# The edge loop of a graph network: two of the four products of a quarter are computed ahead of the previous quarter's sums

## The chip, the cores and the metric

The kernel runs on one core of a Trainium2 chip. The metric is device time in microseconds. The engines are TensorE (PE in the profile; PEld is its load of the stationary operand), ScalarE (ACT), VectorE (DVE), GpSimd (POOL) and SyncE (SP), which issues DMAs. Each engine works through its own instructions strictly in the order written, and waits at a semaphore until another engine has counted it up.

## The reference

The network has 6250 nodes with 256 features and 200,000 edges, sorted by destination. A first layer is a weighted sum over the edges, a linear map and a norm, and gives `x1`. The second layer holds the work of the edge loop:

```
npj  = relu(layer_norm(x1 @ Wp + bp) * gp + betap)               # 20 per node
kron = outer(npj[src], npj[dst]).reshape(E, 400)                 # per edge
kron = relu(layer_norm(kron @ Wk + bk) * gk + betak)             # 256 per edge
kron_feat = segment_sum(kron, dst)
logits = relu([x1[dst], x1[src]] @ We + be)
a = softmax of logits over the edges of one dst
context = relu(segment_sum((x1 @ Wn + bn)[src] * a, dst))
```

A GRU cell, two norms and a linear map on the nodes end the network.

## The kernel before

After the first layer, a table row is stored for each node (`tab_dram`: its values, its `npj` and its half of the logit), and for each node as a destination the matrix `M[node]` of 21 x 257 (`m_dram`), so that an edge's linear result is its source's 21 numbers times the matrix of its destination.

**The tiles.** The edges are cut into tiles of 128 that belong to one bucket of six nodes. The left factor of a tile's product is 126 x 128: for each edge the 21 numbers, placed at its destination's share of 6 x 21. Sixteen tiles are a group (index `g`), a group has four quarters (`s` = 0 to 3) of four tiles. There are 164 groups, and a pass of the loop does four (`UN`), so that there are 41 passes; VectorE, ScalarE and TensorE end a pass between the quarters s=1 and s=2 of a group.

**One quarter, in order.** GpSimd gathers the sources' rows into `feat` (L804), into one of four buffers, each for a group; SyncE loads the 126 x 257 matrices into `m_ring` (L605), which holds 16, one group; the four of a quarter are loaded anew once TensorE has used all four (L602). VectorE multiplies the rows by the one-hots (`products`, L1507). TensorE turns the four tiles into one PSUM bank (`turn_products`, L1911; the profile puts every turn at L1720), ScalarE copies them to SBUF (`evacuate`, L960). TensorE then does a tile's product (`linear`, L1922; two instructions in the profile for each tile). ScalarE squares and sums its 256 columns for the variance (`square`, L970), then VectorE scales the tile out of PSUM into `hgb` (`scaled`, L1518). Only then is its bank free:

```
def bank_of(i):      return 2 if i == SG - 1 else 1 + i % 3
def last_in_bank(i): return {0: 4, 1: 2, 2: 4, SG - 1: 2}.get(i, 3)
...
past(pe, e_hg, t - last_in_bank(i) + 1)       # in linear(q, j)
```

So there are three banks for the products. Tile i of a group waits for the scaling of the tile three back; exceptions are tile 0, which waits for tile 12 of the group before, tile 1, which waits for tile 15 of the group before (two back), tile 2, which waits for tile 14, and tile 15, which waits for tile 13.

**Around the products.** A group later, VectorE clips the tiles (`clipped`, L1574, four in each quarter), which needs the deviations of the whole group: ScalarE computes them in quarter s=0 with a square root (`deviations`, L976), after a load of its function table. In s=1 it computes the exponentials of the slots (L985, L987), in s=2 those of the rows (L981); these need the other table, which is loaded in s=1. ScalarE also copies sums out of PSUM (`kron_rows`, L998, in s=1; `context_rows`, L993, in s=2). TensorE does the sums of the groups before in `softmax_products`:
- s=0: `turn_slot_logits`, which waits for the accumulators' update on VectorE (`add_slots`, L1562 and L1564); `sum_kron` (L1931); two `sum_context` (L1940)
- s=1: `sum_kron`; `turn_logits`, which waits for ScalarE's slot exponentials (L987)
- s=2: `sum_kron`
- s=3: `sum_kron`, two `sum_context`, `sum_slots` (L1969, L1970), which `add_slots` of the next quarter needs

The order is written out by hand for each engine. TensorE works quarter by quarter: products of tiles 0 and 1, turn of the next quarter's tiles, products of tiles 2 and 3, `softmax_products`. ScalarE: square of tile 0, copy of the turned tiles, square of tile 1, the extra function of this quarter, square of tile 2, exponentials, square of tile 3. VectorE: scaling of tiles 0 and 1, an extra step (`add_slots`, `slot_max` or `row_max`), the `products` of the quarter after next, scaling of tile 2, in s=3 the weighted one-hots, scaling of tile 3, the clipping. When a new group is taken up, which is at the head of s=2, `take_indices` (L1493) hands GpSimd the next indices.

Of the kernel before, what the change touches and what calls it, by code (L numbers as in the profile page):

```python
# [95 lines left out]
def gnn_program(nc, io, V, E, EP):  # L96
# [27 lines left out]
    with ExitStack() as ctx:  # L124
# [706 lines left out]
        def _(act):  # L831
# [123 lines left out]
            def evacuate(q):  # L955
                g, u, s = q
                n = g * ST + s
                act.wait_ge(e_t, n + 1)
                past(act, e_h, (n - 1) * G)
                nc.scalar.activation(prods_t[0:KM, s % 2, :], ps[0:KM, 0, :], ACT.Copy).then_inc(e_at, 1)  # L960

            def square(q, j):
                g, u, s = q
                i = s * G + j
                t = g * SG + i
                act.wait_ge(e_h, t + 1)
                past(act, e_sq, t - 1)
                if i == 0:
                    past(act, e_sd, g - 1)
                nc.scalar.activation(junk[:, i % 2, 0:D], ps[:, bank_of(i), 1:HC], ACT.Square, scale=1.0 / 16,  # L970
                                     accum_out=var[:, u % 2, i:i + 1]).then_inc(e_sq, 1)
# [28 lines left out]
            def edge_functions(it):  # L1000
                for k in range(UN * ST):
                    main, turned = quad(it, k - 2), quad(it, k - 1)
                    if main is None:
                        if turned is not None:
                            evacuate(turned)
                        continue
                    g, u, s = main
                    one, two = earlier(it, main, 1), earlier(it, main, 2)
                    square(main, 0)
                    if turned is not None:  # L1010
                        evacuate(turned)
                    square(main, 1)
                    if s == 0 and one is not None:
                        deviations(one[0], one[1] % 2)
                    if s == 1 and two is not None:
                        kron_rows(two[0])
                    if s == 2 and two is not None:
                        context_rows(two[0])
                    square(main, 2)
                    if s == 1 and two is not None:  # L1020
                        slot_exponentials(two[0], two[1] % 2)
                    if s == 2 and one is not None:
                        exponentials(one[0], one[1] % 2)
                    square(main, 3)

            edge_functions(0)
            with act.Fori(1, NS // UN) as it:
# [688 lines left out]
        def _(pe):  # L1716
# [274 lines left out]
            def edge_products(it):  # L1991
                for k in range(UN * ST):
                    turned, main = quad(it, k - 1), quad(it, k - 2)
                    if main is not None:
                        linear(main, 0)
                        linear(main, 1)
                    if turned is not None:
                        turn_products(turned)
                    if main is not None:
                        one, two = earlier(it, main, 1), earlier(it, main, 2)  # L2000
                        if main[2] == 2 and two is not None:
                            turn_slot_exponentials(two[0])
                        if main[2] == 3 and one is not None:
                            turn_exponentials(one[0])
                        linear(main, 2)
                        linear(main, 3)
                        softmax_products(it, main)

            pe.wait_ge(n_ma, 5 * NT)
# [97 lines left out]
```

## Time and profile before

| | |
|---|---|
| median of 3 runs | 9654.78 us (9641.32 to 9657.46) |
| profiled execution: its time / its span | 9633.56 / 9632.1 us |
| mean granted TensorE clock over the span | 0.851 |
| busy over the span | PE 72%, VectorE 64%, GpSimd 48%, ScalarE 39% |
| edge loop | about 4924 to 8773 us |
| middle of the edge loop, 3550 us | PE busy 2679.42, VectorE 2846.37, ScalarE 1975.19, GpSimd 2449.06 us |

The page gives the span in 40 slices, with the loop in slices 20 to 36. Busy time counts work and not waits. TensorE's durations are modelled and overlap, so that starts are the better measure there: the interval between two starts is what a group of instructions takes when nothing waits. A timeline merges neighbouring instructions of one line, and names at the end of a row what ended the idle time before it. In it, one tile's product is 2 instructions of L1922, one `sum_kron` 8 of L1931, one `sum_context` 8 of L1940, and one square an ACTIVATE and a short read of the accumulator.

### The profile page before, as it was taken

To read this page: it belongs to the slowest core of one execution; us is meant where nothing else is said; L and a number is where in the kernel's file an instruction comes from. 1 tells how busy PE (TensorE), PEld (TensorE's weight loads), DVE (VectorE), ACT (ScalarE), POOL (GpSimd) and SP (SyncE) were. 2 spreads that over 40 slices of the span, in tenths; PEclk is the share of its full clock that TensorE was granted. 3 is DMA by queue.
4 is the path that set the end of the run, shared out by engine and by line. 5 is a ranking of instruction groups with operands and counts; after the bars stand their busy time and mean duration, and the time that the engine had idled before them with its cause. 6 is when DMAs were issued, how large, how long until landed. Compare 5 with 4: busy or idle time off the path is not lost.

```text
span 9632.1 us, 164904 instructions
## 1 busy us (share of the span) xinstructions
PE 6952.0 (72%) x33451; PEld 4356.7 (45%) x33452; DVE 6131.5 (64%) x17345; ACT 3717.6 (39%) x10449; POOL 4601.2 (48%) x4921
## 2 busy tenths in 40 slices
PE   3164666666666799988877777777777777777887
PEld 3122444444444577743334444444444444444444
DVE  8894444444444566644458878787888778785555
ACT  0001444444444200023335555555555555553333
POOL 0003777787788400000047666676666666673000
PEclk9586777778787899965569999999999999999888
DMA  0003322222222388854467777777777777775000
GB/s 12 0 0 98 102 93 92 91 91 92 95 91 91 116 263 262 263 190 201 189 212 208 198 197 197 196 203 193 198 199 199 196 196 202 194 201 139 15 16 15
DMA packets 807298, 1398.58 MB, mean 145 GB/s; under 512 B 212677, under 2 KB 578772, under 8 KB 794073
## 3 DMA queue, kind: packets, MB, share of 16 engines
q1 hardware_dynamic: 588922, 797.11, 26.9%
q0 software_dynamic: 215360, 596.47, 21.9%
q14 instruction: 418, 3.42, 0.1%
q10 hardware_dynamic: 2586, 1.37, 0.1%
q8 instruction: 12, 0.20, 0.0%
HBM read 985.87 MB, written 434.45 MB: 147 GB/s over the span
## 4 chain that ended last, share of the span: by engine, by line
PE 32%; issue 22%; DVE 17%; POOL 9%; ACT 8%; DMA 7%; SPq 3%; DVEq 2%; ACTq 1%; POOLq 0%
POOL msg_dram L783 8%; PE ps L1922 7%; PE ps L1720 4%; PE ps L1823 4%; ACT junk L970 3%; PE ps L1940 3%; DMA arena_e<-msg_dram 3%; PE ps L1931 3%; DMA arena_n<-rec_dram 2%; PE ps L1838 2%; DVE arena_e L1574 2%; DVE arena_r L1256 2%; DVE arena_e L1518 2%; SPq L529 2%; ACT L985 1%
## 5 line engine op out<-in xcount | busy, mean ns | idle before, releaser
L804 POOL DMA_INDIRECT arena_n<-tab_dram,idxs x2624 | 2637.6, 1005 | 2831.1 <-DVE idxs L1493 1685.4
L783 POOL DMA_INDIRECT msg_dram<-arena_e,idxq x1760 | 1796.2, 1021 | 473.0 <-issue 467.5
L1922 PE MATMUL ps<-arena_n 126*128 126x257 f32 x5232 | 1686.8, 430 | 446.2 <-DVE arena_e L1518 444.7
L1812 PE MATMUL ps<-arena_n,arena_r 128*128 x3520 | 1252.2, 517 | 383.9 <-ACT arena_r L871 383.9
L970 ACT ACTIVATE junk<-ps 128x256 f32<-128x256 f32 x2616 | 995.7, 382 | 1309.4 <-PE ps L1922 1225.8
L1518 DVE TENSOR_TENSOR arena_e<-ps,gkx 128x257 f32<-128x257 f32 x2616 | 1068.5, 422 | 554.6 <-ACT junk L970 540.0
L1922 PEld LDWEIGHTS ps<-arena_n 126*128 126x128 f32 x5232 | 907.2, 203 | 939.3 <-DVE arena_e L1518 790.6
L1812 PEld LDWEIGHTS ps<-arena_n,arena_r 128*128 128x128 f32 x3520 | 864.8, 257 | 657.5 <-issue 502.7
L876 ACT ACTIVATE arena_e<-ps,recq 128x256 f32<-128x256 f32 x1760 | 809.8, 475 | 772.9 <-PE ps L1812 769.0
L1574 DVE SCALAR_TENSOR_TENSOR arena_e<-arena_e,rstd,nbetak_b 128x256 f32<-128x256 f32 x2608 | 1088.4, 480 | 5.7
L1720 PE MATMUL ps<-ident,arena_n 128*126 128x128 f32 (+1 forms) x3109 | 578.3, 294 | 509.9 <-DVE arena_r L1564 252.7
L1823 PE MATMUL ps<-arena_e,oh 128*128 128x256 f32 x3520 | 818.4, 387 | 85.8 <-DVE oh L1301 84.9
L1081 DVE TENSOR_SCALAR recq<-arena_n 128x16 f32 (+1 forms) x440 | 89.5, 203 | 1240.5 <-DMA msg_dram<-arena_e,idxq 1088.7
L1720 PEld LDWEIGHTS ps<-ident,arena_n 128*126 128x126 f32 (+1 forms) x3109 | 429.8, 150 | 759.3 <-issue 690.1
L1823 PEld LDWEIGHTS ps<-arena_e,oh 128*128 128x128 f32 x3520 | 641.0, 190 | 263.1 <-issue 157.3
L1720 PE MATMUL ps<-ident,oh 128*128 128x128 f32 x1760 | 333.5, 320 | 410.3 <-DVE oh L1301 408.3
L960 ACT ACTIVATE arena_n<-ps 126x512 f32<-126x512 f32 x655 | 390.9, 597 | 362.8 <-PE ps L1720 362.8
L970 ACT ACTIVATION_READ_ACCUMULATOR junk<-ps 128x1 f32 x2616 | 530.1, 203 | 0.0
L1720 PEld LDWEIGHTS ps<-ident,oh 128*128 128x128 f32 x1760 | 226.9, 161 | 614.1 <-DVE oh L1301 600.9
L1931 PE MATMUL ps<-arena_e,oh 128*32 128x257 f32 x5216 | 467.6, 404 | 2.3 <-DVE arena_e L1574 0.5
L871 ACT ACTIVATE arena_r<-ps 128x512 f32<-128x512 f32 x440 | 262.8, 597 | 518.9 <-PE ps L1720 517.5
L1507 DVE TENSOR_TENSOR arena_n<-arena_n,oh 128x504 f32<-128x504 f32 x656 | 445.4, 679 | 22.2 <-DMA arena_n<-tab_dram,idxs 18.9
(308 smaller groups left out, 8995.8 us busy)
## 6 DMA issues: line engine op xcount, KB each, us to landing
arena_n<-m_dram SPq DMA_DIRECT2D x2624, 126.5 KB
arena_e<-msg_dram SPq DMA_DIRECT2D x441, 514.0 KB, 4.5
m_dram<-arena_e SPq DMA_DIRECT2D x49, 1413.5 KB, 4.9
m_dram<-arena_e SPq DMA_DIRECT2D x49, 1285.0 KB, 4.5
arena_n<-tab_dram,idxs POOLq DMA_INDIRECT x2624
hist_dram<-arena_r SPq DMA_DIRECT2D x163, 253.0 KB
msg_dram<-arena_e,idxq POOLq DMA_INDIRECT x1760
arena_n<-rec_dram SPq DMA_DIRECT2D x444, 8.0 KB
```

The lines of the kernel that those rows point to most:

```text
L783: nc.gpsimd.indirect_dma_start(out=msg_dram, in_=msgs[:, u, j, :], in_offset=None, out_offset=bass.IndirectOffsetOnAxis(ap=idxq[:, u, j:j ...
L804: nc.gpsimd.indirect_dma_start(out=feat[:, u, i, :], out_offset=None, in_=tab_dram, in_offset=bass.IndirectOffsetOnAxis(ap=idxs[:, u, i:i ...
L876: nc.scalar.activation(msgs[:, u, j, 0:D], ps[:, 2 + j, 0:D], ACT.Copy, scale=recq[:, u, 4 * j + 2:4 * j + 3]).then_inc(m_msg, 1)
L970: nc.scalar.activation(junk[:, i % 2, 0:D], ps[:, bank_of(i), 1:HC], ACT.Square, scale=1.0 / 16, accum_out=var[:, u % 2, i:i + 1]).then_in ...
L1507: tt(prods[:, s % 2, :].rearrange("p (j n a) -> p j n a", j=G, n=BN), feat[:, u, s * G:(s + 1) * G, PS0:PS0 + KA].unsqueeze(2).broadcast_t ...
L1518: tt(hgb[:, u % 2, i, 0:HC], ps[:, bank_of(i), 0:HC], gkx[:, :], ALU.mult).then_inc(e_hg, 1)
L1574: stt(out=h, in0=h, scalar=rstd[:, u % 2, i:i + 1], in1=nbetak_b[:, :], op0=ALU.mult, op1=ALU.max).then_inc(e_clip, 1)
L1720: return nc.tensor.transpose(out, src, ident[:, :])
L1812: mm(ps[:, 2 + j, 0:D], oh_t[:, q, j * P:(j + 1) * P], at(x_all, nt[u], D, MSG), start=True, stop=True).then_inc(m_x, 1)
L1823: ins = mm(ps[:, q, 0:D], oh[:, q, j * P:(j + 1) * P], msgs[:, u, j, 0:D], start=(j == 0), stop=(j == G - 1))
L1922: mm(ps[:, bank_of(i), 0:HC], prods_t[0:KM, s % 2, j * P:(j + 1) * P], m_ring[0:KM, i, :], start=True, stop=True).then_inc(e_h, 1)
L1931: mm(ps[32 * j:32 * (j + 1), 4, 0:MSG], oh[:, u, 32 * i:32 * (i + 1)], hgb[:, u % 2, i, 1:1 + MSG], start=(s == 0), stop=(s == ST - 1)).th ...
```

## The change

TensorE does the products of tiles 0 and 1 of a quarter not at the quarter's start, but in the quarter before, behind the products of that quarter's tiles 2 and 3 and ahead of its `softmax_products`. ScalarE squares these two tiles at the end of the quarter before. VectorE's order, the number of instructions, the banks and all DMAs stay as they are.

```
@@ edge_functions(it), ScalarE
                     if main is None:
                         if turned is not None:
                             evacuate(turned)
+                            square(turned, 0)
+                            square(turned, 1)
                         continue
                     g, u, s = main
                     one, two = earlier(it, main, 1), earlier(it, main, 2)
-                    square(main, 0)
-                    if turned is not None:
-                        evacuate(turned)
-                    square(main, 1)
+                    evacuate(turned)
                     if s == 0 and one is not None:
                         deviations(one[0], one[1] % 2)
...
                     square(main, 3)
+                    square(turned, 0)
+                    square(turned, 1)
@@ edge_products(it), TensorE
                     turned, main = quad(it, k - 1), quad(it, k - 2)
-                    if main is not None:
-                        linear(main, 0)
-                        linear(main, 1)
                     if turned is not None:
                         turn_products(turned)
                     if main is not None:
...
                         linear(main, 2)
                         linear(main, 3)
+                    if turned is not None:
+                        linear(turned, 0)
+                        linear(turned, 1)
+                    if main is not None:
                         softmax_products(it, main)
```

`main` is the quarter whose tiles VectorE scales in this step, `turned` the next one.

## Rows read from the trace of the kernel before

**Rows 1.** The stretch view, in the middle of the edge loop.
```profile
5100.00:8650.00 3550.00, 2679.42 (x18174) 1665.50 (x18172) 2846.37 (x8177) 1975.19 (x6667) 2449.06 (x2439) 0.95 0.74 198
```

**Rows 2.** The waits, 5100 to 8650 us: total, times, longest.
```profile
DVE arena_e L1518 <- ACT junk L970: 494.2, 691, 2.5
...
DVE idxs L1493 <- issue: 125.4, 38, 4.4
```

**Rows 3.** The timeline of VectorE, one period: start, duration, instruction, idle before it.
```profile
7003.08 0.43 DVE L1518 TENSOR_TENSOR arena_e<-ps,gkx 128x257 f32<-128x257 f32 x1 [1.27 <-ACT junk L970]
7004.30 0.43 DVE L1518 TENSOR_TENSOR arena_e<-ps,gkx 128x257 f32<-128x257 f32 x1 [0.79 <-ACT junk L970]
...
7006.28 0.79 DVE L1518 TENSOR_TENSOR arena_e<-ps,gkx 128x257 f32<-128x257 f32 x2
...
7010.32 0.42 DVE L1518 TENSOR_TENSOR arena_e<-ps,gkx 128x257 f32<-128x257 f32 x1 [0.43 <-ACT junk L970]
...
7013.10 0.43 DVE L1518 TENSOR_TENSOR arena_e<-ps,gkx 128x257 f32<-128x257 f32 x1 [0.45 <-ACT junk L970]
...
7019.92 0.74 DVE L1518 TENSOR_TENSOR arena_e<-ps,gkx 128x257 f32<-128x257 f32 x2
...
7021.97 0.43 DVE L1518 TENSOR_TENSOR arena_e<-ps,gkx 128x257 f32<-128x257 f32 x1
...
7025.15 0.43 DVE L1518 TENSOR_TENSOR arena_e<-ps,gkx 128x257 f32<-128x257 f32 x1 [1.18 <-ACT junk L970]
```

**Rows 4.** The timeline of TensorE, the same period.
```profile
7005.77 0.30 PE L1720 MATMUL ps<-ident,arena_n 128*126 128x128 f32 x1 [1.51 <-DVE arena_r L1564]
7006.01 0.83 PE L1931 MATMUL ps<-arena_e,oh 128*32 128x257 f32 x8
...
7007.63 1.14 PE L1922 MATMUL ps<-arena_n 126*128 126x257 f32 x4
7008.61 0.60 PE L1720 MATMUL ps<-ident,arena_n 128*126 128x128 f32 x4
...
7020.72 0.70 PE L1922 MATMUL ps<-arena_n 126*128 126x257 f32 x2 [1.36 <-DVE arena_e L1518]
7021.35 0.64 PE L1931 MATMUL ps<-arena_e,oh 128*32 128x257 f32 x8
...
7023.79 1.03 PE L1922 MATMUL ps<-arena_n 126*128 126x257 f32 x4
```

**Rows 5.** The timeline of ScalarE, the same period.
```profile
7005.79 0.36 ACT L970 ACTIVATE junk<-ps 128x256 f32<-128x256 f32 x1
...
7009.33 0.60 ACT L960 ACTIVATE arena_n<-ps 126x512 f32<-126x512 f32 x1 [0.48 <-PE ps L1720]
...
7010.18 0.39 ACT L998 ACTIVATE arena_e<-ps 128x257 f32<-128x257 f32 x1
7010.44 0.40 ACT L970 ACTIVATE junk<-ps 128x256 f32<-128x256 f32 x1
...
7010.95 1.28 ACT L985 ACT_TABLE_LOAD   x1
...
7012.60 0.38 ACT L970 ACTIVATE junk<-ps 128x256 f32<-128x256 f32 x1
...
7025.38 0.60 ACT L960 ACTIVATE arena_n<-ps 126x512 f32<-126x512 f32 x1 [0.35 <-PE ps L1720]
7025.87 0.38 ACT L970 ACTIVATE junk<-ps 128x256 f32<-128x256 f32 x1
...
7026.36 1.28 ACT L976 ACT_TABLE_LOAD   x1
...
7027.86 0.36 ACT L970 ACTIVATE junk<-ps 128x256 f32<-128x256 f32 x1
```

**Rows 6.** The groups by line, 5100 to 8650 us: GpSimd's gathers.
```profile
L804 POOL DMA_INDIRECT arena_n<-tab_dram,idxs x2439 | 2450.8, 1005 | 1101.2 <-issue 663.2 <-PE ps L1940 418.2 <-DVE idxs L1493 19.8
```

**Rows 7.** The timeline of TensorE where the loop starts its next pass.
```profile
7080.85 2.08 PE L1922 MATMUL ps<-arena_n 126*128 126x257 f32 x4 [0.40 <-DVE arena_e L1518]
```

More of the change, by code:

```diff
@@ L1005, in edge_functions @@
                             evacuate(turned)
+                            square(turned, 0)
+                            square(turned, 1)
                         continue
@@ L1008, in edge_functions @@
                     one, two = earlier(it, main, 1), earlier(it, main, 2)
[L1009 to L1012, printed above, removed]
+                    evacuate(turned)
                     if s == 0 and one is not None:
@@ L1024, in edge_functions @@
                     square(main, 3)
+                    square(turned, 0)
+                    square(turned, 1)
             edge_functions(0)
@@ L1993, in edge_products @@
                     turned, main = quad(it, k - 1), quad(it, k - 2)
-                    if main is not None:
-                        linear(main, 0)
-                        linear(main, 1)
                     if turned is not None:
@@ L2006, in edge_products @@
                         linear(main, 3)
+                    if turned is not None:
+                        linear(turned, 0)
+                        linear(turned, 1)
+                    if main is not None:
                         softmax_products(it, main)
```

## The prediction

> **What bounds the kernel now.** The views were read in this order: the page's slices, which put the edge loop at 4924 to 8773 us; the stretch view of its middle; the waits there; then the timelines of three engines over one group, side by side. In 3550 us of the loop VectorE is busy 2846 us and TensorE 2679 us, at a granted clock of 0.95 [rows 1], so neither is full, and the loop is a chain that goes round between engines. The stretch holds 2439 gathers [rows 6], 16 to a group: 152.4 groups, 23.3 us each. VectorE, the fullest in its own work, waits 494 us for ScalarE's squares and 125 us (38 times, once a pass) at the head of a pass [rows 2].
>
> One group in steady state lasts 7025.15 - 7003.08 = 22.07 us [rows 3]. VectorE stands idle in it at tile 0 of s=0 (1.27 us), tile 1 of s=0 (0.79), tile 1 of s=1 (0.43), tile 3 of s=1 (0.45): 2.94 us. The first three come from one pattern: TensorE does those products only after the sums of the quarter before. From 7021.35 to 7023.79 it does the sums of s=3, and from 7005.77 to 7007.63 those of s=0 [rows 4], then come the products, the squares and the scalings. Quarters s=2 and s=3 have no wait on VectorE.
>
> **The change part by part.** It removes and adds no instruction. It moves two products of a quarter (TensorE) and their two squares (ScalarE). No DMA is moved, but SyncE's loads and GpSimd's gathers hang on TensorE's counts, see below. In the sum, times of s=0 stand one period (22.07 us) on, where that is needed.
>
> *Product of tile 0, ahead.* Its bank waits for the scaling of tile 1 of the same quarter (in s=3: tile 12), which is over when the product of tile 3 is. It costs its place, 0.44 us, which is not new work. Price 0.
>
> *Product of tile 1, ahead.* Here a wait comes. Its bank is that of tile 2 of the running quarter, and before s=0 that of tile 15, the group's last, which VectorE scales as the last before its clipping. The sums, the next turn, and the next products 2 and 3 are queued behind it on TensorE; ScalarE's copy waits for the turn, and VectorE for both. Step by step, for the two quarters in which it matters:
>
> s=3. The scaling of tile 15 starts at 7021.97 and takes 0.43 [rows 3]; a product that waited for a scaling started 0.06 after that one's end (7019.92 + 0.74 = 7020.66, then 7020.72), and what stood behind it began 0.63 later (7021.35) [rows 3, 4]. So the sums begin at 7021.97 + 0.43 + 0.06 + 0.63 = 7023.09 and not at 7021.35. They take 7023.79 - 7021.35 = 2.44, and the turn of the next quarter then follows at once, at 7025.53. Now two products (0.87, or 0.44 each) stand between, and it starts at 7024.66 (0.72 ahead of ScalarE's copy at 7025.38). The turn is 0.87 late. ScalarE's copy starts 0.72 after the turn (7008.61, 7009.33) [rows 4, 5]. There the change gives something back: behind the copy stood the square of tile 1, 7025.38 to 7026.36 up to the table load. Now the load follows the copy, which is 0.60 long, so at about 0.62 after its start: 0.36 saved. From the table load over the square root to the square of tile 2 it is 7027.86 - 7026.36 = 1.50, and the scaling of tile 2 follows 0.49 after its square (7005.79, 7006.28) [rows 3, 5]. It comes 0.51 later than now, and the waits of tiles 0 and 1 (2.06 us) have only moved to tile 2: VectorE has nothing else to do there but the accumulators and the multiplication.
>
> From scaling to scaling: 0.49 + 0.63 + 2.44 + 0.72 + 0.62 + 1.50 + 0.49 = **6.89 us** from tile 15 to tile 2 of s=0 (now 6.38).
>
> s=0. Tile 1 of s=1 waits for this scaling: 0.49 + 0.63. The sums then take 1.62 without a wait (7006.01 to 7007.63) and 1.86 with one (from 7005.77) [rows 4]; the turn of the slot logits now finds its operands ready, so I take 1.70. The turn, and 0.72 later the copy (0.49 to the next, 7025.38 to 7025.87), the rows' copy (0.26, 7010.18 to 7010.44), the square of tile 2 up to the table load (0.51), from there over two exponentials to the square of tile 3 (1.65, 7010.95 to 7012.60), and 0.50 to the scaling at 7013.10 [rows 3, 5]. Sum: 0.49 + 0.63 + 1.70 + 0.72 + 0.49 + 0.26 + 0.51 + 1.65 + 0.50 = **6.95 us**, where now it is 7013.10 - 7006.28 = 6.82.
>
> s=1, after tile 3, to tile 3 of s=3: VectorE works without a wait, 7021.97 - 7013.10 = **8.87 us** [rows 3], now and then. Products 0 and 1 of s=2 and s=3 wait too, but the turns there lie well ahead of VectorE's clipping, so nothing hangs on them. If that cover were gone, 0.4 to 1 us a quarter would be at stake.
>
> The round is 6.89 + 6.95 + 8.87 = 22.71 against 22.07: **+0.64 us a group**, and 163 groups have it: +104 us.
>
> *Against it: the extra waits.* Over the stretch VectorE waits 494.2 / 152.4 = 3.24 us a group, 0.30 more than the 2.94 of the steady group. Some of it comes from stretches at the lower clock: where the loop starts its next pass, four instructions took 2.08 us [rows 7] instead of about 1.03. In s=2 two products done ahead hide that; in s=3 and s=0 more of TensorE's work lies on the chain. Bounds 0 and -0.30; I take the middle, -0.15, or -25 us.
>
> *The transfers.* SyncE may reload a quarter of the ring once its fourth product is done. In s=1 that is before its scaling at 7013.10, and the first product of s=1 comes again at 7007.63 + 22.07 = 7029.70 [rows 3, 4]: over 16.6 us. In the new order it comes 2 to 3 us sooner, so some 14 us are left. The nearest rows of such size, in the page's list of DMA issues, are transfers of 514 KB that landed in 4.5 us; four matrices are 506 KB. Price 0; the cover is gone if four took over 14 us. GpSimd's gathers cost 2450.8 us and 663.2 us between them, for 152.4 groups 20.4 us a group [rows 6], less than 22.7. The heads of the passes, 3.3 us, hide TensorE's and ScalarE's own. Price 0.
>
> Sum: 104 - 25 = +79 us. For the profiled execution 9633.56 + 79 = about 9712; it stands 21 us under the median of the runs, to which the difference is added: 9654.78 + 79 = **9733 us**. Its bounds: each waiting product 0.44 instead of 0.63 (-0.38 a group), sums of s=0 at 1.62 or 1.86 (-0.08, +0.16), extra waits hidden whole or not at all (-0.15, +0.15): -0.61 to +0.31 a group about the +0.49, so -20 to +130 us.
>
> **The rivals.**
>
> *The banks are free in time (faster).* If product 1 did not wait, the sums of s=3 would start 0.87 after the product of tile 3, the turn would be where it is now, and ScalarE would save its 0.36. In s=0 the two products would lie in the wait for the accumulators, and the turn would come at 7007.7 instead of 7008.61; with 0.36 more saved there, the round is 1.3 us shorter: -212 us, 9443. It would have its place in the waits of products for VectorE. The two waits together cost about 1.97 us; the change gains from where they are below 1.3. Against it stand the scalings of tile 15 and tile 2, which lie 0.6 us and more behind TensorE [rows 3, 4]. Chance 0.08.
>
> *It cancels.* Waiting products restart at 0.44, and all the extra waits go: +0.64 - 0.38 - 0.30 = -0.04 a group, -7 us, 9648. A single row stands for the 0.63. Chance 0.14.
>
> *The clock falls more often.* The granted clock is 0.95 in the stretch [rows 1], so about a tenth of it is at 1.2 GHz. On the new chain lie 0.63 + 2.44 + 0.63 + 1.70 = 5.4 us of TensorE's work a group. The new order gives TensorE a wait in each quarter. If the lower clock held a fifth more of the time, it would be +1.1 us a group, +176 us on top: 9909; a tenth more, 9820. For it: rows 7, after a head. Against: the waits of now are as many (1.51, 1.36 us) [rows 4], and the clock stayed. Chance 0.07. The Trainium skill, "TensorE: Matmul & The Clock Gate", section "HAM oscillation — how this bites in real kernels", says that a loop whose waits starve TensorE each time round falls back to the half clock each time; that rule speaks against this change, and by it the time would be this rival's. The rows at 0.95 bear it out only at the heads.
>
> *The matrices come late.* If four took over 14 us, the excess would be paid up to four times a group. Chance 0.03, some 9800 us.
>
> **How the numbers follow.** The forecast has 0.68, the others 0.08, 0.14, 0.07 and 0.03. 0.2% (19 us) is about what a measurement of this kernel can tell from no change. Slower by more: the forecast's case but for its lower end (0.63), the clock, the matrices, 0.01 of the cancelling case: 0.74. Within: 0.10 of the cancelling case and 0.05 of the forecast's: 0.15. Faster: the free banks (0.08) and 0.03 of the cancelling case: 0.11. The likeliest case's own range is 9680 to 9775. Down to 9630 the range takes in the cancelling case, up to 9800 part of the clock's; the fast rival (0.08) and the worst of the clock stay out.
>
> **What would show it.** Right: VectorE's waits at tiles 0 and 1 of s=0 and tile 1 of s=1 gone, new ones at tile 2 of s=0 (about 1.9 us) and tile 3 of s=1 (over 1 us); product 1 waiting for VectorE ahead of the sums; the table load right behind the copy; a steady group of 22.7 us. Wrong: a steady group under 22 us; ScalarE's table load somewhere else in its order; TensorE's clock well off 0.95; a wait for a DMA ahead of a product.

## The result and the profile after

The changed kernel takes 9793.61 us (median of 4 runs, 9781.63 to 9802.1), the kernel before, run beside it, 9655.23 (4 runs, 9641.32 to 9657.46). The ratio is 1.0145 (95% interval 1.0128 to 1.0163): 138 us slower, where 79 were forecast. The profiled execution lasts 9796.8 us, its span 9795.3, 163 us more than that of before. Behind the change the line numbers are one higher: the product is L1923, the scaling L1519, the turn L1721, the sums L1932 and L1941, the accumulators L1563 and L1565, the clippings L1575. ScalarE's lines are the same.

The page of the changed kernel, its 40 slices; the edge loop fills slices 20 to 36:

```profile
PE   3164666666666799988877777777777777777888
...
DVE  8894444444444566644467777777777777776555
...
PEclk9586777777777899955579989998999999899988
```

TensorE and VectorE show 7 tenths through the loop, as before neither is full. The stretch view of the changed kernel, 5100 to 8650 us, with the columns of [rows 1]:

```profile
5100.00:8650.00 3550.00, 2711.81 (x17506) 1512.98 (x17504) 2713.18 (x7873) 1912.49 (x6413) 2343.20 (x2347) 0.91 0.70 191
```

2347 gathers at 16 to a group are 146.7 groups, 24.2 us each, against 23.3 before. VectorE did less in the same time (2713 against 2846 us), and TensorE, which did 4% fewer instructions, was busy longer: the granted clock is 0.91, not 0.95. The waits of the changed kernel in this stretch, in the form of [rows 2]:

```profile
PEld ps L1923 <- DVE arena_e L1519: 1180.9, 947, 4.6
ACT arena_n L960 <- PE ps L1721: 935.2, 475, 4.2
...
DVE arena_e L1519 <- ACT junk L970: 471.5, 416, 1.7
...
DVE arena_r L1563 <- PE ps L1971: 179.6, 146, 2.9
...
DVE idxs L1494 <- issue: 82.2, 36, 2.8
```

VectorE's wait for squares comes 416 times instead of 691, but each is longer, and one a group for the accumulators has joined it (146 times). ScalarE waits 935 us for the turn, where it waited 304 before. No product waits for a transfer. The wait at the head of a pass has gone down from 125.4 us in 152.4 groups [rows 2] to 82.2 in 146.7: from 0.82 to 0.56 us a group.

VectorE's timeline of the changed kernel, two groups. The first scaling shown of each is tile 15; then come the accumulators, tile 2 of s=0, and tile 3 of s=1:

```profile
6933.31 0.43 DVE L1519 TENSOR_TENSOR arena_e<-ps,gkx 128x257 f32<-128x257 f32 x1
...
6937.20 0.48 DVE L1563 SCALAR_TENSOR_TENSOR arena_r<-arena_r,keep,ps 126x257 f32<-126x257 f32 x1 [1.23 <-PE ps L1971]
...
6940.16 0.79 DVE L1519 TENSOR_TENSOR arena_e<-ps,gkx 128x257 f32<-128x257 f32 x2 [1.36 <-ACT junk L970]
...
6947.00 0.43 DVE L1519 TENSOR_TENSOR arena_e<-ps,gkx 128x257 f32<-128x257 f32 x1 [1.00 <-ACT junk L970]
...
6955.70 0.43 DVE L1519 TENSOR_TENSOR arena_e<-ps,gkx 128x257 f32<-128x257 f32 x1
...
7003.85 0.42 DVE L1519 TENSOR_TENSOR arena_e<-ps,gkx 128x257 f32<-128x257 f32 x1
...
7007.77 0.48 DVE L1563 SCALAR_TENSOR_TENSOR arena_r<-arena_r,keep,ps 126x257 f32<-126x257 f32 x1 [1.25 <-PE ps L1971]
...
7010.69 0.79 DVE L1519 TENSOR_TENSOR arena_e<-ps,gkx 128x257 f32<-128x257 f32 x2 [1.33 <-ACT junk L970]
...
7018.99 0.43 DVE L1519 TENSOR_TENSOR arena_e<-ps,gkx 128x257 f32<-128x257 f32 x1 [1.71 <-ACT junk L970]
...
7027.69 0.43 DVE L1519 TENSOR_TENSOR arena_e<-ps,gkx 128x257 f32<-128x257 f32 x1
```

The waits at tiles 0 and 1 of s=0 [rows 3] are gone; in their place VectorE waits 1.25 us at the accumulators and 1.33 at tile 2. The two groups differ in one segment: from tile 2 to tile 3 of s=1 the first takes 6.84 us, the second 8.30.

TensorE's timeline of the changed kernel, the same two groups:

```profile
6933.79 0.70 PE L1923 MATMUL ps<-arena_n 126*128 126x257 f32 x2 [0.59 <-DVE arena_e L1519]
...
6940.64 0.70 PE L1923 MATMUL ps<-arena_n 126*128 126x257 f32 x2 [1.67 <-DVE arena_e L1519]
6941.18 0.27 PE L1721 MATMUL ps<-ident,arena_n 128*126 128x128 f32 x1
6941.38 0.64 PE L1932 MATMUL ps<-arena_e,oh 128*32 128x257 f32 x8
6941.84 1.05 PE L1941 MATMUL ps<-arena_n,ohx 128*32 128x257 f32 x16
6942.82 0.66 PE L1721 MATMUL ps<-ident,arena_n 128*126 128x128 f32 x4
...
7004.33 0.70 PE L1923 MATMUL ps<-arena_n 126*128 126x257 f32 x2 [0.83 <-DVE arena_e L1519]
7004.96 0.64 PE L1932 MATMUL ps<-arena_e,oh 128*32 128x257 f32 x8
...
7011.18 0.70 PE L1923 MATMUL ps<-arena_n 126*128 126x257 f32 x2 [1.67 <-DVE arena_e L1519]
7011.72 0.27 PE L1721 MATMUL ps<-ident,arena_n 128*126 128x128 f32 x1
7011.92 0.79 PE L1932 MATMUL ps<-arena_e,oh 128*32 128x257 f32 x8
7012.47 1.96 PE L1941 MATMUL ps<-arena_n,ohx 128*32 128x257 f32 x16
7014.35 1.11 PE L1721 MATMUL ps<-ident,arena_n 128*126 128x128 f32 x4
```

Both groups have the wait that the change brings: the product of tile 1 waits for VectorE's scaling ahead of the sums, 0.59 and 0.83 us in s=3 and 1.67 in s=0 of both. In s=0 it is 1.67 us in each of the 156 groups counted below; in s=3 it is 0.59 in 130 of them. After it the first group's 16 context products take 1.05 us and the second's 1.96. The windows view of the changed kernel over these sums and what follows, columns as in [rows 1], shows the clock:

```profile
7012.47:7017.34 4.87, 4.54 (x31) 2.58 (x23) 3.88 (x14) 1.74 (x5) 3.65 (x5) 0.67 0.85 237
6941.84:6946.05 4.21, 3.18 (x30) 1.68 (x22) 3.89 (x14) 2.45 (x6) 3.29 (x4) 1.00 0.99 242
```

The third number from the end is the granted clock: 1.00 in the first group, and 0.67 in the second, a mixture of 2.4 and 1.2 GHz. ScalarE's timeline of the changed kernel, in the second group:

```profile
7008.09 0.60 ACT L960 ACTIVATE arena_n<-ps 126x512 f32<-126x512 f32 x1 [2.55 <-PE ps L1721]
7008.70 1.28 ACT L976 ACT_TABLE_LOAD   x1
...
7010.21 0.36 ACT L970 ACTIVATE junk<-ps 128x256 f32<-128x256 f32 x1
...
7015.59 0.60 ACT L960 ACTIVATE arena_n<-ps 126x512 f32<-126x512 f32 x1 [3.20 <-PE ps L1721]
```

The table load stands right behind the copy (0.61 after its start; 0.98 before, from 7025.38 to 7026.36 in [rows 5]).

**All groups.** One group is one sample, so the table is worked out from the starts of all of VectorE's scalings in the trace, for groups 5 to 160 (156 groups): the time from one scaling to the next one named, mean, and in brackets lowest / median.

| us | tile 15 to tile 2 of s=0 | to tile 3 of s=1 | to tile 15 | group |
|---|---|---|---|---|
| before | 6.42 (6.39 / 6.39) | 6.75 (6.70 / 6.74) | 10.28 (8.85 / 8.88) | 23.44 (21.96 / 22.16) |
| changed | 6.92 (6.84 / 6.85) | 7.80 (6.84 / 8.38) | 9.63 (8.69 / 8.75) | 24.35 (22.38 / 24.07) |
| difference of means | +0.50 | +1.05 | -0.65 | +0.91 |
| difference of lowest | +0.46 | +0.14 | -0.16 | +0.42 |

0.91 us in 163 groups is 148 of the 163 us between the two profiled executions. (Between the medians of the runs it is 138; the profiled execution of the kernel before lay 21 us under its median.) The lowest values show the chain without disturbance: +0.42 a group, or +0.44 as the sum of the three segments. Above the lowest, the means of before lie 0.03, 0.05 and 1.43 us, those of the changed kernel 0.08, 0.96 and 0.94. So the third segment has lost 0.49 of its disturbances, and the second has gained nearly all of its own. What that 0.96 is, a split of the segment by the granted clock inside it shows:

| segment to tile 3 of s=1 | clock full: groups, us | clock fallen: groups, us |
|---|---|---|
| before | 139, 6.75 | 17, 6.73 (mean clock 0.97) |
| changed | 61, 6.84 | 95, 8.42 (mean clock 0.80) |

The 95 groups pay 1.58 us each: 95 / 156 of 1.58 is 0.96. The 17 of before are hardly comparable: none of them has a mean clock under 0.95. Where the fall begins tells more. In all 95 groups the low clock begins 0.6 to 1.6 us after the start of tile 2's scaling, and the product that waited for this scaling starts 0.48 after it; so the clock falls within 1.2 us of the end of that wait. In the kernel before it begins there in no group.

The loss of disturbances in the third segment can be located, too. Where a pass's head lies in the segment (every fourth group), its mean went from 13.69 to 12.17 us, which is 0.34 of the 0.49 in the mean over all groups; in the other groups it went from 9.15 to 8.78, which is the remaining 0.15.

### The profile page after: what moved, and what is told of

Read it like the earlier page. It is cut to its first block, busy times and chain, and to the rows that moved or that the text cites. A ratio compares the mean times of both kernels' runs of the same rounds, so it can differ in the third digit from the quotient of the medians.

```text
span 9795.3 us, 164959 instructions
## 1 busy us (share of the span) xinstructions
PE 7089.9 (72%) x33455; PEld 4254.9 (43%) x33456; DVE 6106.4 (62%) x17345; ACT 3731.4 (38%) x10453; POOL 4609.7 (47%) x4921
## 4 chain that ended last, share of the span: by engine, by line
PE 27%; issue 23%; DVE 20%; POOL 10%; ACT 8%; DMA 7%; SPq 2%; DVEq 2%; ACTq 1%; POOLq 0%
POOL msg_dram L783 9%; PE ps L1824 4%; PE ps L1941 4%; DVE arena_e L1575 4%; PE ps L1923 4%; PE ps L1721 3%; DVE arena_e L1519 3%; DMA arena_e<-msg_dram 3%; PE ps L1932 3%; ACT junk L970 2%; ACT L976 2%; PE ps L1839 2%; DVE arena_r L1257 2%; DMA arena_n<-rec_dram 2%; SPq L529 1%
## 5 line engine op out<-in xcount | busy, mean ns | idle before, releaser
L1923 PE MATMUL ps<-arena_n 126*128 126x257 f32 x5236 | 1667.1, 429 | 924.1 <-DVE arena_e L1519 919.8
L783 POOL DMA_INDIRECT msg_dram<-arena_e,idxq x1760 | 1821.0, 1035 | 473.0 <-issue 463.6
L1923 PEld LDWEIGHTS ps<-arena_n 126*128 126x128 f32 x5236 | 892.6, 201 | 1478.5 <-DVE arena_e L1519 1329.8
L1519 DVE TENSOR_TENSOR arena_e<-ps,gkx 128x257 f32<-128x257 f32 x2616 | 1024.2, 419 | 565.2 <-ACT junk L970 529.5
L1575 DVE SCALAR_TENSOR_TENSOR arena_e<-arena_e,rstd,nbetak_b 128x256 f32<-128x256 f32 x2608 | 1090.3, 480 | 5.7
L1721 PE MATMUL ps<-ident,oh 128*128 128x128 f32 x1760 | 337.5, 323 | 432.6 <-DVE oh L1302 430.8
L1721 PE MATMUL ps<-ident,arena_n 128*126 128x128 f32 (+1 forms) x3109 | 561.7, 302 | 38.9 <-DVE arena_n L1508 18.6
L1721 PEld LDWEIGHTS ps<-ident,arena_n 128*126 128x126 f32 (+1 forms) x3109 | 384.9, 152 | 341.7 <-issue 310.2
L1721 PEld LDWEIGHTS ps<-ident,oh 128*128 128x128 f32 x1760 | 227.5, 162 | 637.9 <-DVE oh L1302 625.6
L1932 PE MATMUL ps<-arena_e,oh 128*32 128x257 f32 x5216 | 487.1, 448 | 0.2 <-DVE arena_e L1575 0.2
```

Source lines behind the costliest of these rows:

```text
L783: nc.gpsimd.indirect_dma_start(out=msg_dram, in_=msgs[:, u, j, :], in_offset=None, out_offset=bass.IndirectOffsetOnAxis(ap=idxq[:, u, j:j ...
L1519: tt(hgb[:, u % 2, i, 0:HC], ps[:, bank_of(i), 0:HC], gkx[:, :], ALU.mult).then_inc(e_hg, 1)
L1575: stt(out=h, in0=h, scalar=rstd[:, u % 2, i:i + 1], in1=nbetak_b[:, :], op0=ALU.mult, op1=ALU.max).then_inc(e_clip, 1)
L1721: return nc.tensor.transpose(out, src, ident[:, :])
L1923: mm(ps[:, bank_of(i), 0:HC], prods_t[0:KM, s % 2, j * P:(j + 1) * P], m_ring[0:KM, i, :], start=True, stop=True).then_inc(e_h, 1)
L1932: mm(ps[32 * j:32 * (j + 1), 4, 0:MSG], oh[:, u, 32 * i:32 * (i + 1)], hgb[:, u % 2, i, 1:1 + MSG], start=(s == 0), stop=(s == ST - 1)).th ...
```

## The experiments

Two theories stood after the result. One: the longer chain (product 1 waits, and all behind it) explains the loss, and ScalarE's new order only gives 0.36 us back. The rival: the loss is chiefly that the clock falls at the new wait. The kernels below undo one half of the change each, do it for one tile, feed TensorE in the wait, or take the wait away.

On two of the three chips that the experiments ran on, the kernel before itself took 11586 to 11787 us, and a group of the kernels below lasted 32.6 to 35.8 us in the mean, so that the totals there say little about this change. Two things are compared from them. One is the first segment, tile 15 to tile 2 of s=0, in groups at full clock; it seems not to depend on the chip, since the changed kernel with products added behind this segment has 6.85 us there as the changed kernel has in the result (the kernel before was not traced on those chips). The other is whether the low clock begins within 2 us of the start of tile 2's scaling, as it does in 95 of the 156 groups of the changed kernel:

| kernel | product of tile 1 in s=0 waits | groups of 156 in which the clock falls there |
|---|---|---|
| before | not ahead of the sums | 0 |
| changed (two executions) | 1.67 us | 95, 99 |
| TensorE's half alone (two) | 1.28 us | 88, 83 |
| ScalarE's half alone (two) | not ahead of the sums | 0, 0 |
| tile 0 alone ahead (two) | not ahead of the sums | 0, 0 |
| changed, TensorE fed in the wait (three) | TensorE is busy instead | 0, 0, 0 |
| changed, deviations moved | 0.05 to 0.29 us | 0 |
| ScalarE's half, deviations moved | not ahead of the sums | 0 |

**TensorE's half alone.** ScalarE keeps the order of before.

```
@@ ScalarE: as before
@@ TensorE: as changed
-                    if main is not None:
-                        linear(main, 0)
-                        linear(main, 1)
...
+                    if turned is not None:
+                        linear(turned, 0)
+                        linear(turned, 1)
```

> TensorE's new order alone; ScalarE squares where it did before (tile 0, copy, tile 1). Theory A (the loss is the wait of product 1 ahead of the sums, and ScalarE's new order gives back 0.36 us behind the copy in s=0 and in s=1): slower than the changed kernel by about 0.7 us a group, some 9910 us. Theory B (the squares at the end of a quarter are what costs, TensorE's order is harmless): at or below 9655 us.

> TensorE's new order alone, again, since in the run before all engines of the chip had long waits for instructions (34 us a group in place of 22 to 24), also in the kernel before. Theory A (the loss is the wait of product 1 ahead of the sums, and ScalarE's new order gives back 0.36 us in s=0 and in s=1): slower than the changed kernel by about 0.7 us a group, 2.5 to 3% over the kernel before. Theory B (the squares' new place costs): at or below the kernel before.

Measured 12094.68 us against 11753.52 (1.0293, 1.0274 to 1.0312) on one chip, 11955.69 against 11586.3 (1.0324, 1.0307 to 1.0341) on another. In total that is a little more than the 2.5 to 3% expected. At full clock the segment is 7.21 us in 116 groups and 7.22 in 104. VectorE's and ScalarE's timelines of the second run:

```profile
7985.88 0.43 DVE L1518 TENSOR_TENSOR arena_e<-ps,gkx 128x257 f32<-128x257 f32 x1
...
7991.11 0.42 DVE L1518 TENSOR_TENSOR arena_e<-ps,gkx 128x257 f32<-128x257 f32 x1 [2.89 <-ACT junk L970]
...
7993.09 0.79 DVE L1518 TENSOR_TENSOR arena_e<-ps,gkx 128x257 f32<-128x257 f32 x2
```

```profile
7990.11 0.60 ACT L960 ACTIVATE arena_n<-ps 126x512 f32<-126x512 f32 x1 [3.70 <-PE ps L1720]
7990.61 0.38 ACT L970 ACTIVATE junk<-ps 128x256 f32<-128x256 f32 x1
...
7991.10 1.28 ACT L976 ACT_TABLE_LOAD   x1
```

Behind the late copy ScalarE still has the square of tile 1 (7990.61) ahead of its load. TensorE's half costs 7.21 - 6.39 = 0.82 us here, and the changed kernel, at 6.85, has 0.36 of it back. The rest of this kernel's loss is not split up; the fall of the clock is in it (88 and 83 groups).

**ScalarE's half alone.** TensorE keeps the order of before (behind the loop it does the last pass's two products for ScalarE).

```
@@ ScalarE: as changed
-                    square(main, 0)
-                    if turned is not None:
-                        evacuate(turned)
-                    square(main, 1)
+                    evacuate(turned)
...
+                    square(turned, 0)
+                    square(turned, 1)
@@ TensorE: as before, and after the loop
+            linear((NS - 1, 3, 2), 0)
+            linear((NS - 1, 3, 2), 1)
```

> ScalarE's new order alone; TensorE does products 0 and 1 behind the sums as before (and two products after the loop, whose squares ScalarE now waits for). Theory A: the copy and the table load no longer stand behind the square of tile 1, so the chain is 0.36 us shorter in s=0 and in s=1, and the accumulators' update comes about 0.85 us sooner: a steady group of about 20.9 us, the time some 9460 us (9430 to 9560). Theory B (the squares' new place costs): 9700 us or more. If ScalarE's order hardly matters: 9655 us.

> ScalarE's new order alone, again. Theory A: the copy and the table load no longer stand behind the square of tile 1, the chain is 0.36 us shorter in s=0 and in s=1 and the accumulators' update comes about 0.85 us sooner: a steady group of about 20.9 us, a ratio of 0.975 to 0.99. Theory B: 1.005 or more.

Measured 11706.05 us (0.9961, 0.9944 to 0.9978) and 11610.63 (1.002, 1.0007 to 1.0033). The expected gain (9430 to 9560 us, a ratio of 0.975 to 0.99) did not come, and the two chips disagree in sign. The segment at full clock is 6.04 us in 41 groups and 6.03 in 54. VectorE's timeline of the second run, tile 15 and tile 2:

```profile
7645.65 0.42 DVE L1519 TENSOR_TENSOR arena_e<-ps,gkx 128x257 f32<-128x257 f32 x1
...
7651.68 0.79 DVE L1519 TENSOR_TENSOR arena_e<-ps,gkx 128x257 f32<-128x257 f32 x2 [0.58 <-ACT junk L970]
```

6.39 - 6.03 = 0.36: the same 0.36, on the other side. Whether this half alone makes the whole kernel faster stays open; in 115 and 102 of the 156 groups the clock had fallen within the first segment, which then took 7.5 to 7.6 us.

**Tile 0 alone ahead.** Product and square of tile 1 stay where they were.

```
@@ ScalarE
-                    square(main, 0)
-                    if turned is not None:
-                        evacuate(turned)
-                    square(main, 1)
+                    evacuate(turned)
+                    square(main, 1)
...
+                    square(turned, 0)
@@ TensorE
-                        linear(main, 0)
...
+                    if turned is not None:
+                        linear(turned, 0)
+                    if main is not None:
                         softmax_products(it, main)
```

> Only tile 0's product goes ahead of the sums, and only its square to the end of the quarter; tile 1 stays behind the sums. Its bank is free when TensorE comes to it, so nothing waits. Theory A (only the wait of product 1 costs): no loss, and no gain either, since the turn and the copy come when they did: a steady group of 22.1 us, 9655 us within 30. Theory C (any product put ahead of the sums delays the chain): about half of the loss, 9725 us.

> Only tile 0's product and square go ahead, again. Theory A (only the wait of product 1 costs): a steady group of 22.0 us, as before, a ratio of 1.00 within 0.003. Theory C (any product ahead of the sums delays the chain): 1.007.

Measured 11812.04 us (1.0051, 1.0032 to 1.0069) and 11553.14 (0.9971, 0.9959 to 0.9984); segment 6.36 us in 124 groups of each run, before 6.41 at full clock. Expected were a ratio of 1.00 within 0.003 by one theory and 1.007 by the other; the two runs lie on either side of 1. VectorE's timeline of the second run:

```profile
7812.42 0.42 DVE L1518 TENSOR_TENSOR arena_e<-ps,gkx 128x257 f32<-128x257 f32 x1
...
7818.78 0.79 DVE L1518 TENSOR_TENSOR arena_e<-ps,gkx 128x257 f32<-128x257 f32 x2
```

So tile 0 ahead costs nothing in this segment, as the prediction had it: the 0.82 is tile 1's.

**TensorE fed in the wait.** The changed kernel with 13 more products between tile 0 and tile 1 in s=0; what they write is overwritten unread.

```
+            def fill(n):
+                for _ in range(n):
+                    mm(ps[:, 0, 0:P], ident[:, :], iota[:, :], start=True, stop=True)
...
                         linear(turned, 0)
+                        if main is not None and main[2] == 0:
+                            fill(13)
                         linear(turned, 1)
```

> The changed kernel with 13 extra 128-column products (about 0.11 us each, 1.43 us in all) into the turned tiles' bank, between products 0 and 1 ahead of the sums of s=0, where TensorE waits 1.67 us now; their results are overwritten unread. Theory A with the clock (the groups of 24.0 us are those of 22.4 us with the clock fallen after that wait): most groups go back to 22.4 us, the granted clock in the loop rises from 0.91 towards 0.97, and the time falls by 100 to 200 us, to 9600 to 9700 us. Without the clock (the chain alone is the loss): 9794 us or slightly more.

> The changed kernel with 13 extra 128-column products in TensorE's wait of s=0, again. Theory A with the clock: most groups of 24.0 us go back to 22.4, the granted clock in the loop rises from 0.91 towards 0.97, a ratio of 0.995 to 1.005 to the kernel before, where the changed kernel had 1.0145. Without the clock: 1.0145 or slightly more.

> The changed kernel with 13 extra 128-column products in TensorE's wait of s=0, meant for a chip without the holds. By the clock: the segment from tile 2 of s=0 to tile 7 (s=1), 8.38 us in the median after the change and 6.84 at best, is 6.84 in nearly all groups, as it was when the deviations were moved and with them most of that wait; the time falls by about 1 us a group against the changed kernel, to a ratio of about 1.00 to the kernel before. If the fallen clock is not what makes the segment long: 8.4 us stays, ratio 1.016 or more. If the extra products get in the way, the segment is over 6.84 by a constant in all groups.

Measured 11959.68 us (1.0185, 1.0164 to 1.0207), 11833.38 (1.0218, 1.0199 to 1.0236) and 11970.7 (1.0159, 1.0132 to 1.0186), all on the two chips with long groups; none of the expected gains came. TensorE's timeline of the first of the three, and its windows view from tile 2's scaling (7494.00) on, columns as in [rows 1]:

```profile
7492.65 3.07 PE L1994 MATMUL ps<-iota,ident 128*128 128x128 f32 x26
7495.55 0.60 PE L1923 MATMUL ps<-arena_n 126*128 126x257 f32 x2
```

```profile
7494.00:7497.00 3.00, 3.00 (x35) 2.43 (x37) 2.90 (x9) 0.70 (x4) 2.11 (x3) 1.00 0.61 146
```

The filling was mis-sized. The expectations took 0.11 us for each of 13 products, 1.43 in all; but each is two instructions in the profile, and the 26 take 2.90 us (7492.65 to 7495.55) in each of the 156 groups of each run. That is longer than the wait of 1.67: the product of tile 1 now starts 1.55 us after tile 2's scaling has started, and not 0.48, so that 1.07 us of new delay stand ahead of the sums. The second segment lasts 13.4 to 14.0 us in the mean, where the other kernels on those chips have 11.4 to 12.7. The totals therefore cannot show what the clock gives back.

What these runs do show is the cause of the fall. With TensorE busy in place of the wait, and the rest of the program as in the changed kernel, the clock falls within 2 us of tile 2's scaling in none of 3 x 156 groups. TensorE's half alone, with a wait of 1.28 us at that place, has the fall in 88 and 83 of 156 on the same two chips. With the filling the clock falls only later in the segment, 5.2 us or more behind tile 2's scaling, as it also does with tile 0 alone ahead; TensorE is then held between its context products, which is peculiar to these chips. Over the loop (6500 to 10500 us) the granted clock was 0.82 to 0.84, against 0.73 to 0.79 in the others there. The price by this test, with a filling that fits the wait and on a chip like that of the result, was not measured.

**The changed kernel again**, on a third chip.

```
(no edit)
```

> The changed kernel itself, for its ratio beside the runs on the chips where TensorE is held for several microseconds in the sums (34 us a group). The segment from the scaling of tile 15 to that of tile 2 of s=0, which that hardly touches, should be 6.85 us, as in the profile after. Its ratio by theory A: between the one of TensorE's half alone (1.03) and 1.00, so about 1.015 to 1.02; if the waits there hide the chain, 1.00.

Measured 9798.71 us against 9639.56 (7 runs), 1.0158 (1.0141 to 1.0175). Segments 6.91, 7.83, 9.62, group 24.37; the second is 6.84 in 57 groups at full clock and 8.42 in 99 with the clock fallen (mean 0.80). The ratio is in the expected 1.015 to 1.02. The pattern belongs to the kernel, not to one execution.

**The wait taken away.** The chain from the copy to tile 2 of s=0 holds the table load and the square root of `deviations`, 1.50 us in the prediction. Here they are moved to the end of s=3, before the copy is due; all else is the changed kernel.

```
                     evacuate(turned)
-                    if s == 0 and one is not None:
-                        deviations(one[0], one[1] % 2)
...
                     square(main, 3)
+                    if s == 3:
+                        deviations(g, u % 2)
                     square(turned, 0)
                     square(turned, 1)
```

> The changed kernel, with the deviations of a group (the load of the square root's table, and the root) moved from s=0, behind the copy, to the end of s=3, behind the square of tile 15. Theory A (from tile 15 to tile 2 the chain goes over the product of tile 1, the sums of s=3, turn, copy, table load, square of tile 2): 1.50 us of it go, the square of tile 2 follows the copy by 0.49, and the segment falls from 6.85 to about 5.3 us, bounded by VectorE's own accumulators and multiplication behind the sums (3.56 + 1.66 = 5.2). The time falls by up to 1.5 us a group (2% and more on a chip without the holds). Rival D (VectorE's scaling of tile 2 waits for the product and not for ScalarE): the segment stays at 6.85.

Measured 9458.09 us (9452.65 to 9476.98) against the same 9639.56: 0.9816 (0.9797 to 0.9835), faster than either kernel. Its stretch view (5100 to 8400 us), VectorE's, TensorE's and ScalarE's timelines:

```profile
5100.00:8400.00 3300.00, 2573.95 (x17865) 1453.19 (x17863) 2757.62 (x8039) 1930.87 (x6545) 2382.88 (x2399) 0.96 0.77 210
```

```profile
6950.24 0.43 DVE L1519 TENSOR_TENSOR arena_e<-ps,gkx 128x257 f32<-128x257 f32 x1
...
6955.48 0.79 DVE L1519 TENSOR_TENSOR arena_e<-ps,gkx 128x257 f32<-128x257 f32 x2
...
6962.32 0.42 DVE L1519 TENSOR_TENSOR arena_e<-ps,gkx 128x257 f32<-128x257 f32 x1 [1.00 <-ACT junk L970]
```

```profile
6935.16 0.70 PE L1923 MATMUL ps<-arena_n 126*128 126x257 f32 x2 [0.22 <-DVE arena_e L1519]
...
6954.20 2.46 PE L1923 MATMUL ps<-arena_n 126*128 126x257 f32 x8
```

```profile
6954.48 0.60 ACT L960 ACTIVATE arena_n<-ps 126x512 f32<-126x512 f32 x1 [1.93 <-PE ps L1721]
6954.98 0.38 ACT L970 ACTIVATE junk<-ps 128x256 f32<-128x256 f32 x1
```

Tile 2 now comes 5.24 us after tile 15, and the product of tile 1 waits 0.22 us in s=0 in the first row of TensorE, and too little to show in the second (eight products' instructions in one row); over all groups it is 0.05 to 0.29. In all 156 groups the clock stays full through the second segment, and it takes 6.83 us. The segments are 5.50 (5.23 / 5.41), 6.83 (6.83 / 6.83), 9.84 (8.69 / 8.74), the group 22.18. Against the changed kernel run beside it this is 1.41 us off the first segment and 1.00 off the second, where the edit removes nothing and the undisturbed value is the same (6.83 and 6.84): that 1.00 is the clock's. The third segment is 0.22 us longer than in the changed kernel.

**ScalarE's half with the deviations moved**, TensorE as before.

```
@@ on ScalarE's half alone
-                    if s == 0 and one is not None:
-                        deviations(one[0], one[1] % 2)
...
                     square(main, 3)
+                    if s == 3:
+                        deviations(g, u % 2)
```

> TensorE's old order, ScalarE's new one, and the deviations at the end of s=3. Theory A: no product waits ahead of the sums, and neither the squares nor the table load stand between copy and scaling. Tile 15 to tile 2: bounded by VectorE, tile 1 at 3.55 us, accumulators and multiplication behind it, 5.5 us (6.39 before). Tile 2 to tile 7: 6.35 us (6.74 before). Tile 7 to 15: 8.7 to 8.9. A steady group of about 20.7 us, as short as the changed kernel with the deviations moved (20.8 to 21.0): a ratio of 0.97 to 0.985. If TensorE's new order were of use by itself, this one would be slower than that by several tenths of a us a group.

Measured 11696.84 us against 11786.71 (0.9918, 0.989 to 0.9945), on a chip with long groups; 0.97 to 0.985 was expected. The segment is 5.36 us in 53 groups at full clock, and 6.88 in the 103 others. At full clock the kernel above has 5.37 (142 groups), so with the load out of the way TensorE's order makes no difference to this segment. What the two would be worth against each other as whole kernels, on a chip with short groups, was not measured. Nor was the kernel before with nothing but the deviations moved, so how much of the gain of 1.8% needs the new order at all is open.

## Why the prediction was right in its direction and short in its size

Forecast +79 us, measured +138. The time lies in the range, 9630 to 9800, near its end; it is outside the likeliest case's own range (9680 to 9775). That it lies in the range is partly luck. The clock's 0.96 us a group, which the sum had at nothing, is 156 us by itself and would have put the forecast at 9889; a chain and disturbances smaller than taken brought the time back.

- **The chain, tile 15 to tile 2: right.** 6.84 to 6.85 us for a forecast of 6.89, term by term in the group at 6933.31: 4.24 to the copy (4.28), 0.61 to the load (0.62), 1.51 to the square (1.50), 0.49. The halves run alone confirm the two parts: TensorE's +0.82, ScalarE's -0.36. VectorE's waits add up to 2.58 us, 2.57 in the working (2.06 and 0.51); the sign named for it, about 1.9 us at tile 2, does not follow from that working, and was 1.33 to 1.36. That nearly half of the wait would stand at the accumulators, which wait for the sums as well, was not foreseen.
- **Product of tile 0: right** at nothing (6.36 us with it alone ahead).
- **Tile 2 to tile 3 of s=1, at full clock: nearly right.** 6.84 for 6.95. The single row for a waiting product (0.63 to what stands behind it) was too dear for s=0, where it is 0.54 (6940.64 to 6941.18); in s=3, where it was read, it is 0.63 still (7004.33 to 7004.96). The turn follows 1.64 after that, not 1.70.
- **The rest of the group:** said to be unchanged at 8.87, it is 8.70. Steady group 22.39 for 22.71; the chain is +0.44, not +0.64.
- **"Against it: the extra waits": mis-sized.** -0.15 us a group was taken, within bounds of 0 and -0.30. The third segment's mean fell by 0.49 more than its undisturbed value, beyond the bound. It is 0.34 in the groups with a pass's head, where the wait itself shrank by 0.26 (0.82 to 0.56), and 0.15 in the others; why these run more smoothly was not found.
- **"The clock falls more often": this is the step that failed.** The sum has no term for it: the clock's price was put at nothing, where the runs show 0.96 us a group. As a rival it was given 0.07, with the reason that waits of 1.51 and 1.36 us were there before and the clock stayed. The fact was right: in the kernel before TensorE waits 1.50 to 1.61 us for the accumulators in s=0, and the clock stays full behind it in all 156 groups. The inference was not: in TensorE's half alone a shorter wait, of 1.28 us, is followed by the fall in more than half of them. The length of that one wait does not decide it.

  The change puts a wait of 1.67 us in s=0 ahead of the sums, and in 95 of 156 groups the clock is low right behind it, where sums and turn lie on the chain. In the group at 7010.69 the sums take 2.63 instead of 1.64 us, the turn 1.24 instead of 0.77 to the copy, and all else is as long as ever: 8.30 for 6.84.

  Over the stretch the clock went from 0.95 to 0.91. A granted clock of 0.95 is 0.10 of the time at 1.2 GHz, one of 0.91 is 0.18. The rival's own price for a tenth more was +0.54 a group; these eight hundredths cost 0.96, so both its chance and its price were low; its sign, a clock well off 0.95, was seen. The price spread the low clock evenly over the group; it falls where the chain runs through TensorE. The Trainium skill, "TensorE: Matmul & The Clock Gate", section "HAM oscillation — how this bites in real kernels", describes a loop whose wait for data in each round is longer than TensorE's work in it, and says that it gets the half clock anew in every round. The trace agrees with it in 95 groups of 156, and not in the 61 others, which have the same wait at a granted clock of 1.00. But this loop is not the page's case: TensorE is busy in 2712 of 3550 us here, so the prediction leaned on that rule further than it reaches.

Put together, a group: +0.44 for the chain, -0.49 for the smaller disturbances of the third segment, +0.96 for the clock: +0.91. The forecast had +0.64, -0.15 and nothing: +0.49.

That TensorE's wait ahead of the sums is what lets the clock fall is shown from two sides: with TensorE busy in it the clock stays full there in 468 of 468 groups, and with the wait nearly taken away in 156 of 156. The price is shown by the split (1.58 us for each group hit) and by the kernel with the deviations moved (1.00 us a group). Why 61 groups with the wait keep the clock, and why the wait of before never loses it, stays open. The other rivals did not come: no bank was free in time, no matrix late.

## What to carry to other kernels

Work moved ahead on an in-order engine is free only if what it waits for is done by then: here one product of 0.44 us held up the sums and the turn behind it, which the next stage waited for. Ask of a wait put into TensorE's order not only how long it is but what stands right behind it, since that work may run at half clock; price the low clock at the work of the chain that it hits, not as an average. Then look for what else is on the new chain: moving one table load and its square root out of it turned a loss of 1.6% into a gain of 1.8%. And when you fill a wait, read from a trace what one filling instruction takes and how many instructions a product is, or the filling becomes a delay of its own.

## What the runs showed of the hardware

- The same wait of 1.67 us on TensorE was followed by the full clock in 61 groups and by a fallen one in 95; 57 and 99 in the other execution. With a wait of 1.28 us there it was fallen in 88 and 83. With TensorE kept busy in the wait it fell there in none of 468, and behind waits of 1.50 to 1.61 us for the accumulators, in the kernel before, in none of 156.
- A wait for a scaling ended with the product's start 0.47 to 0.48 us after the scaling's start. The instruction behind the product's pair began 0.54 us later where it was a turn, and 0.63 where it was a sum.
- A product of 128 x 128 by 128 columns in f32 was two instructions in the profile; 13 of them took 2.90 us at full clock, 0.11 us for each instruction.
- On two chips the kernel before took 11586 to 11787 us, where it took 9640 on a third and 9655 in the runs of the result; groups of the other kernels lasted 32.6 to 35.8 us on those two. ScalarE's timeline of the kernel with tile 0 ahead shows one of the holds:

```profile
8117.09 0.60 ACT L960 ACTIVATE arena_n<-ps 126x512 f32<-126x512 f32 x1 [7.30 <-remote]
```

The context products of that quarter had started by 8110.14, and their completions arrived one by one from 8112.55 to 8116.31; in the kernel before, on the chip of the result, products started at 7006.46 to 7007.32 were complete at 7007.07 to 7007.72. What holds them there was not found.
